# The band mask of a windowed attention: added by TensorE in the accumulator, or by VectorE in place

## What is computed

```python
q, k, v = split(x @ Wqkv);  q = l2norm(q) * qs;  k = l2norm(k) * ksc   # then rotary on q and k
it, jb = query index, key index                   # 32 queries x 64 keys in a window
mask = (it < jb) | (it > jb + w) | (jb == -1)
sim = einsum('bhwie,bhwje->bhwij', bq, bk2) * 8.0
sim = where(mask, -finfo.max, sim)
out = einsum('bhwij,bhwje->bhwie', softmax(sim), bv2);  x = out @ Wo + x
```

## Time and profile before

| | us |
|---|---|
| median of 3 runs | 6815.98 |
| lowest, highest | 6815.96, 6818.55 |
| the profiled execution: its own time | 6810.38 |
| its span, first to last instruction | 6808.3 |
| PE matmul busy, weight loads busy | 5859.0, 3846.0 |
| DVE, ACT, POOL busy | 4950.7, 3279.8, 2894.9 |
| band matmuls (line 600) | 384 |
| maximum and subtraction (lines 839, 843) | 192 each |

### The profile page before, as it was taken

One profiled execution on the slowest core, in us unless ns is written; L12 is line 12 of the kernel. 1 busy time (PEld: TensorE's weight loads), 2 busy tenths in 40 slices (PEclk: granted clock), 3 DMA queues, 4 the chain that ended last, 5 costly groups with the idle time before them and its releaser, 6 DMA issues. The chain is left out here.

```text
span 6808.3 us, 141874 instructions
## 1 busy us (share of the span) xinstructions
PE 5859.0 (86%) x47596; PEld 3846.0 (56%) x47596; DVE 4950.7 (73%) x9384; ACT 3279.8 (48%) x7050; POOL 2894.9 (43%) x3503
## 2 busy tenths in 40 slices
PE   4776898999999978888988988998699898989897
PEld 1223666666666654575566566566466566656565
DVE  5995666666666646998998998998566666666664
ACT  3334666666666652222222222222466666666664
POOL 1443555555555531222122122122455555555553
PEclk7998999999999988988998998998899999999999
DMA  0001222222222210000000000000122222222221
GB/s 15 0 0 50 60 65 67 58 66 58 66 60 64 57 32 14 1 1 1 1 0 1 0 1 1 0 1 1 52 59 67 66 59 65 60 64 61 63 57 38
DMA packets 163232, 246.83 MB, mean 36 GB/s; under 512 B 36981, under 2 KB 57393, under 8 KB 162487
## 3 DMA queue, kind: packets, MB, share of 16 engines
q1 hardware_dynamic: 162614, 238.71, 13.4%
HBM read 36.20 MB, written 1.05 MB: 5 GB/s over the span
## 5 line engine op out<-in xcount | busy, mean ns | idle before, releaser
L1347 PE MATMUL psum<-tk_kT,tk_qs 128*128 128x512 f32 (+3 forms) x4128 | 1266.2, 468 | 9.2 <-POOL tk_qs L1580 9.2
L1580 POOL TENSOR_TENSOR tk_qs<-tk_qT,tk_mix 128x1024 f32<-128x1024 f32 x258 | 498.4, 1935 | 1550.0 <-PE psum L1348 1416.3
L1347 PEld LDWEIGHTS psum<-tk_kT,tk_qs 128*128 128x128 f32 x4128 | 762.4, 209 | 437.8 <-issue 294.6
L869 POOL TENSOR_TENSOR f_rope<-f_rope,f_t 128x1024 f32<-128x1024 f32 x384 | 908.0, 2364 | 119.8 <-DVE f_t L788 118.1
L473 PE MATMUL psum<-f_wqkv,f_xs 128*128 128x512 f32 x1536 | 769.1, 624 | 106.9 <-DMA f_wqkv<-in_Wqkv 94.6
L1537 DVE MAX8 tk_m<-tk_work 128x8 f32<-128x528 f32 (+3 forms) x1792 | 818.1, 496 | 2.2 <-issue 0.9
L882 POOL TENSOR_TENSOR f_rope<-f_rope,f_rn 128x1024 f32<-128x1024 f32 x384 | 731.0, 1904 | 58.4 <-POOL f_rn L861 2.2
L1543 DVE MATCH_REPLACE8 tk_work<-tk_m,tk_work 128x400 f32<-128x400 f32 (+3 forms) x1536 | 744.3, 492 | 0.0
L784 DVE TENSOR_TENSOR f_rope<-psum,f_rot 128x1024 f32<-128x1024 f32 x384 | 469.1, 1222 | 354.4 <-ACT f_sq L717 276.0
L819 DVE TENSOR_TENSOR f_o_tok<-psum,f_rden 128x1024 f32<-128x1024 f32 x192 | 235.1, 1225 | 583.7 <-PE psum L558 583.7
L464 PE MATMUL psum<-ident,f_rope 128*128 128x128 f32 x3072 | 410.8, 278 | 262.1 <-ACT f_probT L634 259.5
(11 more groups left out here) (233 smaller groups left out, 10968.0 us busy)
## 6 DMA issues: line engine op xcount, KB each, us to landing
f_v<-f_v_tok SPq DMA_DIRECT2D x1152, 128.0 KB, 2.4
f_v<-f_v_tok SPq DMA_DIRECT2D x768, 64.0 KB, 2.0
f_wqkv<-in_Wqkv SPq DMA_DIRECT2D x36, 512.0 KB, 5.0
f_wo<-in_Wo SPq DMA_DIRECT2D x12, 512.0 KB, 4.3
f_w<-in_W SPq DMA_DIRECT2D x12, 341.0 KB, 3.2
f_w<-in_W SPq DMA_DIRECT2D x24, 64.0 KB
tk_wkv<-in_Wkv SPq DMA_DIRECT2D x1, 1024.0 KB, 5.8
out<-y_tok SPq DMA_DIRECT2D x4, 256.0 KB, 2.5
```

Of the source, the lines that this page charges most:

```text
L869: pool.tensor_tensor(part, part, t2[:, half, :, :], ALU.add).then_inc(s[f"{name}_added"], 1)
L1347: pe.matmul(psum[:, j, 0:n], qs[:, j, c, :], kT[:, c, 0:n], start=(c == 0), stop=False, skip_group_check=True)
L1580: pool.tensor_tensor(qs[:, j, :, :], qT[:, :, P * t:P * (t + 1)], mix[:, :, heads(p, j)].to_broadcast([P, PAIRS, P]), ALU.mult).then_inc(s ...
```

## The change

In the stacks the two identity matmuls that write the mask are gone, and the score matmuls start their own sums (`start=True`). VectorE adds the mask to both score banks in place, with the band plane broadcast over the two banks, and the maximum waits for that add by a new semaphore, `banded`. Nothing else changes; the band tile, its type and the identity stay.

```diff
@@ names of semaphores
-                  "scores", "top", "sub_done", ...
+                  "scores", "banded", "top", "sub_done", ...
@@ TensorE, step
                         sj = (j - 1) % 4
-                        for half in range(2):
-                            pe.matmul(psum[:, 4 + half, :], k.ident_bf[:, :], k.band[:, int(sj == 0), :, :].rearrange("p h w -> p (h w)"),
-                                      start=True, stop=False, skip_group_check=True)
                         for c in range(PAIRS):
                             for w in range(WPT):
                                 t0 = P * (sj % 2) + WIN * w
                                 last = pe.matmul(psum[WIN * w:WIN * (w + 1), 4 + c // 4, (c % 4) * P:(c % 4 + 1) * P],
                                                  qT[:, c, WIN * w:WIN * (w + 1)], kT[:, c, :, t0:t0 + 2 * WIN],
-                                                 start=False, stop=True, skip_group_check=True)
+                                                 start=True, stop=True)
@@ VectorE, step
                         wait(dve, "scores", through(g, 1))
+                        two_banks = psum[:, 4:6, :].rearrange("p a (h w) -> p a h w", w=2 * WIN)
+                        band = k.band[:, int((j - 1) % 4 == 0), :, :].unsqueeze(1).to_broadcast([P, 2, 8, 2 * WIN])
+                        dve.tensor_tensor(two_banks, two_banks, band, ALU.add).then_inc(s["banded"], 1)
+                        wait(dve, "banded", through(g, 1))
                         dve.tensor_reduce(top[:, :], sc_bank, AX_X, ALU.max).then_inc(s["top"], 1)
```

More of the change, by code:

```diff
@@ L335, in ffn_stack @@
                   "qt0_full", "qt1_full", "qt0_evac", "qt1_evac", "ot0_full", "ot1_full", "ot0_evac", "ot1_evac",
-                  "scores", "top", "sub_done", "exp_done", "summed", "rden_done", "pv_done", "on_done", "wo_full", "wo_evac", "res_done",
+                  "scores", "banded", "top", "sub_done", "exp_done", "summed", "rden_done", "pv_done", "on_done", "wo_full", "wo_evac", "res_done",
                   "ff_in", "ff_mean", "ff_centred", "ff_squared", "ff_var", "ff_x", "ff_logged", "ff_y", "ff_polish", "ff_rstd", "ff_wide", "ff_scaled",
```

## The result

The changed kernel takes 7051.72 us (median of 4 runs, 7041.32 to 7057.46) against 6815.97 us: 3.45% slower, ratio 1.0345 with a 95% interval of 1.0327 to 1.0363, or 236 us. Forecast was 7006, with a range of 6925 to 7085. The profiled execution took 7054.37 us (span 7052.2).

A forecast was written before the change was run, and what follows sets the result against it. Bound: the loop of waits from k turn through scores, VectorE and ACT's exponential back. 6810.4 + 119.6 chain + 37.0 and 33.9 clock = 7000.9, forecast 7006 us since the median of runs stands 5.6 higher; range 6925 to 7085.

The forecast's parts named there:

- What bounds: Loop of k turn (eight transposes of normalised k), tensor work, scores, maximum, subtraction, exponential, ACT; not the 86% busy tensor engine.
- link 1 to 2: Time from step 1's exponential to step 2's: forecast 1.26 - 0.37 = +0.89 us.
- The add's price: VectorE's in-place PSUM add of the mask: 1.225 us, 1.26 with the maximum's wait for it.
- the rival at 2.36 us: In-place add costs 2.36 us: 7143 us without the clock, 7213 with it; chance 6%.
- How much of the 0.52 comes back: Tensor time of the two removed matmuls; the add starts earlier by at most VectorE's idle time before the maximum.
- The sum of the chain: Added exponential-to-exponential time over both stacks, from the add less what comes back: 119.6 us.
- The clock in step 0: Longer tensor idleness makes the granted clock fall in all other 24 step 0s, 1.54 us each: 37.0 us.
- The clock in steps 1 and 2: Half of the 44 step 1s get a clock fall, 22 x 1.54 = 33.9 us; step 2 costed at nothing.
- The clock term as a whole: New half-clock falls in steps 0 and 1 together, 37.0 + 33.9 us; steps 2 and 3 nothing.
- The forecast without a clock term, 6936: Rival: only the chain, clock as before or nearly, 6816 + 119.6 = 6936 us; chance 24%.
- The faster rival: TensorE as the bound: 100 us go, the add lies in VectorE's idle time, 6716 us; chance 4%.
- the one without a change: Rival: every link has the room of link 2 to 3, 17 us or less, 6833 or below; chance 3%.

The follow-up runs named there:

- e1: Kernel before plus VectorE's in-place mask add and its wait, the two band matmuls kept, mask size halved: 7053.31 us, ratio 1.035.
- e7: Changed kernel with idle matmuls in all steps (9, 4, 5, 2) and a second mask add, each with half the mask: 7157.74 us, ratio 1.0497.
- e3: Changed kernel with idle bf16 matmuls (9, 4, 5, 2 in steps 0 to 3) between the turn of the probabilities and the k turn: 6906.14 us, ratio 1.0142.
- e4: Kernel before with idle bf16 matmuls (8, 4, 3, 1 in steps 0 to 3) between the turn of the probabilities and the k turn: 6787.83 us, ratio 0.9959.
- e5: Changed kernel with 9 idle matmuls in step 0 alone, none in the other steps: 6934.84 us, ratio 1.0171.
- e6: Changed kernel with 5 idle matmuls in step 2 alone, none in the other steps: 6973.65 us, ratio 1.0228.
- e2: Changed kernel without VectorE's add and its wait, so no mask is applied at all: 6758.24 us, ratio 0.9916.

## Why the prediction was right, and where not

- **What bounds.** Right. 190 waits of the k turn for ACT are still there (330.4 us); a bare add (e1) lengthens the link 1 to 2 by 1.27 us, and a second one (e7) lengthens every kind of link at full clock by 1.26 or 1.27. One wait on this loop was read over: "almost without gaps" does not hold in step 2, where the third hidden block's matmul waits 1.05 us for VectorE, in the kernel before as in the changed one (44 times, 46.1 us).
- **The add's price.** 1.225 taken, 1.233 measured; 1.26 with its wait, 1.26 measured, and in e7 a second time. Reading and writing PSUM in place took 8 ns more than reading it, so the rival at 2.36 us falls.
- **How much of the 0.52 comes back.** Link 1 to 2: +0.89 forecast, +0.83 measured; 0 to 1 (e3 against e4): 19.83 - 19.08 = +0.75 against +0.74. VectorE gives back some 0.06 more than its idle time says, because the next instruction starts about that much before the one in front has ended (1515.69 + 1.21 = 1516.90, next start 1516.84). 2 to 3: the exponential comes 0.45 later, as worked out; I had booked its slack in this link, but it is used up behind the exponential (there to the probability copy it was 3.56 us and is 3.20) and so shows in the next. 2 to 3 and 3 to 0 together: +0.94 forecast, 0.45 + 0.47 = +0.92 measured.
- **The sum of the chain.** 119.6 us forecast, 118.3 by e3 against e4. The round at full clock, 81.2 forecast, is 81.12. That the sums agree to 1 us is in part luck: by the same two traces the steps without feed-forward work cost 8.2 us where 12.0 was booked, and the links at the layer starts 11.5 where 7.4 was.
- **The clock in step 0.** The right number of steps (all 36), the wrong size: 1.54 us each, taken from the earlier trace rows, where the clock was low for 3.4 us. Now it is low for 6.2 us in the mean, and the link is 22.22 - 19.83 = 2.39 us longer (without the two at the ends of the stacks). All 36 together are 84 us longer than in e3 (793.7 against 709.9), less the 18 of before; I had 37.
- **The clock in steps 1 and 2.** Wrong in place, and with it the sign that the link 2 to 3 would stay unmoved within 0.5 us: that holds for 12 links of 44. I gave step 1 half its links and step 2 none; measured are 0 of 44 and 32 of 44, the latter at 24.08 - 22.52 = 1.56 us, 50 us. For step 1 I had let the whole added wait fall in front of the k turn. It does not: in step 1 ACT evacuates the feed-forward variance right behind the exponential, and the second half of v, one step up in TensorE's list, waits for that evacuation. The k turn's own wait stays at 1.44 us (1.43 in the earlier trace rows). The two waits together are the 2.4 to 2.7 us that I had forecast as one. TensorE in step 1 of the changed kernel:

```profile
1499.62 1.45 PE L473 MATMUL psum<-f_wqkv,f_xs 128*128 128x512 f32 x3
1500.91 1.02 PE L514 MATMUL psum<-f_wqkv,f_xs 128*128 128x512 f32 x2
...
1503.07 1.10 PE L514 MATMUL psum<-f_wqkv,f_xs 128*128 128x512 f32 x2 [1.14 <-ACT f_ffn L669]
...
1506.48 1.06 PE L464 MATMUL psum<-ident,f_rope 128*128 128x128 f32 x8 [1.44 <-ACT f_probT L631]
```

- **The clock term as a whole** was 71 us and is 121 (116 within the stacks): the term of the sum that was mis-sized, too small for the length of the falls in step 0, with the errors in steps 1 and 2 (34 forecast, 50 measured) partly hidden in the total. That the time still lies in the range is in part luck: the term was made of falls in step 1 that did not come and left out those of step 2 that did. The forecast without a clock term, 6936, is 116 us short; the clock costs the changed kernel 145.6 us, 2.1% of 7052. The Trainium skill (TensorE: Matmul & The Clock Gate, section What's actually happening) puts the ramp at under 1% of a typical kernel's span; the figure does not carry over to this kernel, whose clock falls again and again.
- **The faster rival** fell, as did the one without a change: no link got shorter at full clock, apart from those at the layer starts, of which each pair taken together got longer on average (434.3 to 446.1 us for the ten).

What stays open is the rule of the falls, and so why two waits of 1.14 and 1.44 us with 2 us of work between them bring no fall in step 1, and 0.50 and 1.72 in step 2 mostly do. e5 and e6 show that the falls of the other steps take part; how, was not settled.

## What to carry to other kernels

Work moved off the busiest engine is worth what the loop of waits says, not what the busy share says: here the vector engine stood on the loop, so 0.52 us of tensor time, worth 0.43 to 0.54 us a step (e2), was traded for 1.26 us of loop. When a loop through other engines gets longer, the tensor engine idles longer in each turn, and its clock can fall for it; here that second price (121 us) was as large as the first (118 us), and it was found by filling the idle time with useless matmuls. Two kernels with the same total are not two kernels with the same terms (e1); compare step by step at equal clock.

## What had not been expected of the hardware

- More work made the kernel faster: 858 idle matmuls in e3 take off 146 us, and 692 in e4 24 us.
- With the falls of the clock, rounds of different length came out at the same one. At full clock a round of four steps is 81.12 us in the changed kernel's work (e3) and 82.55 in e1 (19.45 + 22.52 + 20.20 + 20.38); with the falls more than half of the rounds of both are 85.2 to 85.4 us long. Why is not shown.
- An in-place add over two PSUM banks with a bf16 broadcast operand takes 1233 ns, against 1225 for one that only reads PSUM (both medians).
